# A transformer with two mixtures of experts: routing weights, expert table and destinations made in the tiles' blocks instead of the routers

## The chip, the cores and the metric

The kernel runs on one core of one Trainium2 chip. The time is the device time of one execution in microseconds (us). The engines are PE (TensorE, matrix products), DVE (VectorE), ACT (ScalarE), POOL (GpSimd) and SP (SyncE, which here only issues DMAs). Each engine runs its own row of instructions in order; they meet through semaphores.

## What is computed

Six residual layers on x, 64 sequences of 32 tokens of 256 values, T = 2048 tokens in all: cross attention with 16 heads, a gated recurrence, a mixture of experts (8 experts, the 2 best for each token, plus a shared one), cross attention with one head, causal attention, and a second mixture (16 experts, the 4 best, plus a shared one). The change is in the two mixtures alone:

```python
# first mixture, after a layer norm
logits = x @ Wg
probs = jax.nn.softmax(logits, axis=-1)
vals, idx = jax.lax.top_k(probs, TOP_K)                       # TOP_K = 2 of E = 8
weights = vals / (jnp.sum(vals, axis=-1, keepdims=True) + EPS)
...
act = jax.nn.silu(hpre)                                       # x @ W1[e] + b1[e]
out = jnp.einsum('te,teh->th', cw, y)                         # y = act @ W2[e] + b2[e]
out = out + SHARED_SCALE * shared
# second mixture, scores = sigmoid(logits)
_, tidx = jax.lax.top_k(masked, TOPK)                         # 4 of 16, from the 2 best groups of 4
w = jnp.take_along_axis(scores, tidx, axis=1)
w = w / (jnp.sum(w, axis=-1, keepdims=True) + 1e-20)          # times 2.5
...
hact = jax.nn.silu(g) * u * combine[:, :, None]
```

## The kernel before

P = 128 is the number of partitions, T = 2048 tokens are NT = 16 tiles of 128, D = 256 is the width, C = 2 its halves. The program is a row of stages, and a stage a row of blocks; at a block's end all engines meet. A mixture has four blocks.

**The boundary** (`boundary`) makes the layer norm, turns it for PE and stores its rows in DRAM (`n_rows`) for the gathers.

**The router** (`route`, L1000 to L1160) sorts tokens by expert. PE makes the logits. DVE makes, in `choose`, the best experts of each token (`r.choice`) and their weights (`r.w`): in the first mixture through ACT's exponential (L1709 to L1719), in the second by picking from the sigmoids (L2207 to L2224). Then, still on DVE and nearly all of it serial (each step signals `m_chain` and the next waits for it): which token has which expert (`hot`, L1082), how many tokens each expert has before and in this place (PE, L1041 and L1042), how many tiles of 128 rows each expert needs (`need`, L1103), where they end (`ends`, the scan of L1105) and begin (`begins`). From `ends` comes the **expert table** `r.expert` (L1110 to L1123): for each routed tile its expert, six of them packed in one integer. From `begins` and `place` comes each token's slot (L1114, L1125 to L1130), cut in tile (`hi_f`) and row (`lo_f`). A loop (L1143 on DVE, L1062 on ACT, L1049 on PE) places the token numbers into slots by one-hot products, and ACT copies the outcome into `halves`. From its differences `held` (L1146) DVE makes the token of each slot (`r.token`, L1153) and the **destinations** `r.dest` (L1148 to L1157): the row of `y_rows` in DRAM where that slot's result goes. The routed tiles number 39 in the first mixture and 79 in the second (`mix.tiles`).

**The tiles** (`first_tiles`, L1188; `second_tiles`, L1402). The loop runs over u = 0 to N-1: the first 16 tiles are the shared expert on the tokens in their order, the others are routed. Per tile PE multiplies up (`ascend`), ACT applies silu, DVE splits the hidden values in two halves of 16 bits (`split` in the first; `multiply`, `high`, `low` in the second), PE multiplies down (`descend`), DVE takes the result (`add` or `result`; L1567 for shared, L1571 for routed tiles of the second). In the second, PE also turns the hidden values (`flip`) and ACT copies them (`flipped`). PE runs ahead of DVE: `ascend(u + 2)` in the first and `ascend(u + 3)` in the second stand before `descend(u)`. Beside the shared tiles ACT and DVE split the experts' weights, which came by DMA during the router, slot by slot (`cast_high` L959, `cast_low` L965). In the second, DVE's order per tile is

```python
for u in range(N):
    if u + 3 < N:
        multiply(u + 3)
        high(u + 3)
        low(u + 3)
    result(u)
    for i in casts(u):
        slots.cast_low(dve, i)
```

and what ties PE to DVE there is, in `descend(u)`, the wait for the product's buffer of two tiles before, `pe.wait_ge(k.t_ycopied.sem, k.t_ycopied.at(u - 1))`, that is `result(u - 2)`.

POOL gathers the routed tiles' rows from `n_rows` (`gather`, L1371 and L1599), by `r.token`, and scatters results to `y_rows` (`scatter`, L1375 and L1603), by `r.dest`. In the first tiles it may be three gathers ahead, in the second 44: there it issues 44 gathers at the block's start before its first scatter. PE and ACT read `r.expert` into registers to find a routed tile's weights (`Experts`).

The combination then adds each token's results with the weights `r.w`.

## Time and profile before

| | |
|---|---|
| median of 3 runs | 1519.88 us (1517.51 to 1522.65) |
| the profiled execution | 1531.23 us |
| its span in the profile | 1529.2 us |
| PE busy (matmuls) | 1169.9 us, 77% of the span |
| DVE busy | 1031.0 us, 67% |
| ACT busy | 826.0 us, 54% |
| POOL busy | 435.7 us, 28% |
| mean granted clock of PE | 0.874 |

The profiled execution stands 11.35 us above the median; 2.0 us of it lie outside the span. An engine can be idle because it waits for another, and a row of the timeline says after its work in brackets how long the engine was idle before and who ended that ("issue": nothing that the profile shows; "remote": an unknown queue). PEclk is the granted clock as a share of 2.4 GHz.

### The profile page before, as it was taken

What the parts mean: (1) busy time and instruction counts of PE and PEld (TensorE: products, weight loads), DVE (VectorE), ACT (ScalarE), POOL (GpSimd) and SP (SyncE); (2) the same over time, 40 slices, a digit from 0 to 9 for tenths busy, and PEclk for the clock granted to TensorE, in tenths of its full rate; (3) what the DMA queues carried; (4) which work ended last, traced back from release to release, by engine and by line L of the source; (5) the groups of instructions that cost most, each with busy time, mean ns of one, the idle gap of its engine ahead of it and who ended that gap; (6) DMA issues with size and microseconds to landing.
All of it is one profiled execution on the core that took longest, in us unless ns stands there. A gap on an engine that the chain in (4) does not pass through costs nothing. (4 is left out here: it accounts for less than half of the span.)

```text
span 1529.2 us, 41178 instructions
## 1 busy us (share of the span) xinstructions
PE 1169.9 (77%) x13430; PEld 862.1 (56%) x13430; DVE 1031.0 (67%) x2885; ACT 826.0 (54%) x2163; POOL 435.7 (28%) x480
## 2 busy tenths in 40 slices
PE   4899999998798539999999927678723327787890
PEld 2688888886344429988888724235611215555660
DVE  5699999997647777966666545345779228454566
ACT  6688888885588546844444306127454125444450
POOL 0555555551200000023333202000200641555550
PEclk9999999999899759999999958789955659899895
DMA  2333333331000283011111169970160320222228
GB/s 95 99 78 80 82 76 81 81 82 64 1 1 1 91 318 155 2 57 47 51 50 51 37 204 321 348 234 1 66 255 28 87 65 19 73 76 78 78 69 281
DMA packets 111934, 151.45 MB, mean 99 GB/s; under 512 B 13632, under 2 KB 96960, under 8 KB 111680
## 3 DMA queue, kind: packets, MB, share of 16 engines
q1 hardware_dynamic: 95792, 114.11, 23.6%
q0 software_dynamic: 11328, 30.95, 6.6%
q10 hardware_dynamic: 4688, 4.72, 0.9%
q8 instruction: 78, 1.28, 0.4%
q14 instruction: 48, 0.39, 0.1%
HBM read 127.97 MB, written 21.76 MB: 98 GB/s over the span
## 5 line engine op out<-in xcount | busy, mean ns | idle before, releaser
L1291 ACT ACTIVATE mixture_and_attentions_h<-ps,mixture_and_attentions_b 128x128 f32<-128x128 f32 x440 | 125.3, 373 | 137.3 <-PE ps L1243 134.3
L1243 PE MATMUL ps<-xture_and_attentions_m_w 128*128 128x128 f16 x1872 | 156.2, 219 | 1.8 <-DVE xture_and_attentions_m_w L1319 1.7
L1243 PEld LDWEIGHTS ps<-xture_and_attentions_m_w 128*128 x1872 | 129.1, 98 | 37.1 <-issue 3.5
L648 POOL TENSOR_TENSOR ads_and_recurrence_ctx_s<-ads_and_recurrence_ctx_c,ads_and_recurrence_ctx_s 128x512 f16<-128x512 f32 x64 | 74.2, 1159 | 178.2 <-ACT ads_and_recurrence_ctx_s L577 178.2
L597 ACT ACTIVATE ads_and_recurrence_probs<-ps,s_and_recurrence_neg_max 128x257 f32<-128x257 f32 x256 | 117.7, 480 | 1.1 <-DVE s_and_recurrence_neg_max L679 1.1
L1261 PE MATMUL ps<-xture_and_attentions_m_w,ixture_and_attentions_hs 128*128 x312 | 117.5, 379 | 1.0 <-DVE xture_and_attentions_m_w L1344 1.0
L1599 POOL DMA_INDIRECT tage_second_mixture_rows<-n_rows,e_second_mixture_r_token x79 | 76.8, 973 | 133.7 <-POOLq L1002 110.0
L1475 PE MATMUL ps<-stage_second_mixture_m_w,stage_second_mixture_x_s 128*128 x474 | 98.5, 348 | 20.7 <-ACT stage_second_mixture_x_s L1517 13.9
L1603 POOL DMA_INDIRECT y_rows<-stage_second_mixture_y,ge_second_mixture_r_dest x79 | 77.1, 976 | 124.6 <-DVE stage_second_mixture_y L1571 114.5
L1371 POOL DMA_INDIRECT ture_and_attentions_rows<-n_rows,e_and_attentions_r_token x39 | 39.0, 999 | 258.1 <-POOLq L1002 159.6
L1327 DVE TENSOR_SCALAR ixture_and_attentions_hs<-mixture_and_attentions_h 128x512 f16<-128x512 f32 x110 | 47.6, 433 | 87.7 <-PE ps L1262 71.3
L1550 DVE SCALAR_TENSOR_TENSOR stage_second_mixture_h<-ps,stage_second_mixture_h 128x192 f32<-128x192 f32 x95 | 33.8, 355 | 97.5 <-ACT stage_second_mixture_h L1522 55.5
L688 DVE TENSOR_SCALAR _heads_and_recurrence_pn<-ads_and_recurrence_probs,heads_and_recurrence_inv 128x256 f32<-128x256 f32 x256 | 79.8, 371 | 8.3
L1262 PE MATMUL ps<-xture_and_attentions_m_w,ixture_and_attentions_hs 128*128 x312 | 85.0, 273 | 0.0
L679 DVE TENSOR_REDUCE s_and_recurrence_neg_max<-ps 128x2 f32<-128x514 f32 x128 | 81.8, 678 | 1.9 <-PE ps L519 1.9
L494 PE MATMUL ps<-ads_and_recurrence_ctx_s,currence_wh_L_xattn_wk_t 128*128 128x256 f16 x512 | 78.3, 276 | 5.1 <-issue 5.1
L1522 ACT ACTIVATE stage_second_mixture_h<-ps 128x192 f32<-128x192 f32 x95 | 31.4, 331 | 90.6 <-PE ps L1475 42.4
L1329 DVE SCALAR_TENSOR_TENSOR ixture_and_attentions_hs<-mixture_and_attentions_h,ixture_and_attentions_hs 128x512 f16<-128x512 f32 x110 | 76.3, 693 | 3.8
L527 PE MATMUL ps<-consts_sb,_heads_and_recurrence_pn 128*128 128x128 f32 x512 | 77.0, 273 | 2.2 <-DVE heads_and_recurrence_p_t L695 2.2
L1490 PE MATMUL ps<-stage_second_mixture_m_w,stage_second_mixture_h_t 128*128 (+1 forms) x95 | 27.4, 288 | 66.1 <-DVE x_sb L1567 30.9
L503 PE MATMUL ps<-currence_wh_L_xattn_wv_t,ads_and_recurrence_ctx_s 128*128 128x256 f16 x512 | 77.7, 275 | 0.0
L1375 POOL DMA_INDIRECT y_rows<-xture_and_attentions_m_w,re_and_attentions_r_dest x39 | 38.5, 986 | 132.6 <-DVE xture_and_attentions_m_w L1344 132.3
(401 smaller groups left out, 3371.9 us busy)
## 6 DMA issues: line engine op xcount, KB each, us to landing
ads_and_recurrence_ctx_t<-in_ctx_t SPq DMA_DIRECT2D x64, 257.0 KB, 2.7
e_and_attentions_b_ctx_t<-in_ctx_t SPq DMA_DIRECT2D x15, 1028.0 KB, 9.1
ure_and_attentions_b_ctx<-in_ctx SPq DMA_DIRECT2D x30, 512.0 KB, 8.9
xture_and_attentions_m_w<-in_m_w SPq DMA_DIRECT2D x2, 5632.0 KB, 37.3
ds_and_recurrence_mask_i<-in_mask SPq DMA_DIRECT2D x256, 32.1 KB, 1.7
tage_second_mixture_rows<-y_rows SPq DMA_DIRECT2D x16, 512.0 KB, 9.6
stage_second_mixture_m_w<-in_m_w SPq DMA_DIRECT2D x2, 3840.0 KB, 20.5
xture_and_attentions_m_w<-in_m_w SPq DMA_DIRECT2D x1, 5120.0 KB, 16.6
```

Of the source, the lines that this page charges most:

```text
L494: last = pe.matmul(ps[:, KB, m * KR:(m + 1) * KR], w[:, c, m * P:(m + 1) * P], x[:, c, :], start=(n_ == 0), stop=(n_ == len(products) - 1))
L503: last = pe.matmul(ps[:, VB, r * D:(r + 1) * D], x[:, c, r * P:(r + 1) * P], w[:, c, :], start=(n_ == 0), stop=(n_ == len(products) - 1))
L527: last = pe.transpose(ps[:, TB, j * P:(j + 1) * P], pn[p][:, j, r * P:(r + 1) * P], c_["ident"])
L597: act.activation(probs[p][:, j, :], ps[:, SB + j, 0:SK], ACT.Exp, bias=neg_max[:, p, j:j + 1], accum_out=sums[:, p, j:j + 1]).then_inc(k.a ...
L679: dve.tensor_reduce(neg_max[:, p, 2 * h:2 * h + 2], ps[:, SB + 2 * h:SB + 2 * h + 2, 0:SK], AX.X, ALU.max, negate=True).then_inc(k.a_max.s ...
L688: last = dve.tensor_scalar(pn[p][:, j, :], probs[p][:, j, 0:KR], inv[:, p, j:j + 1], None, ALU.mult)
L1243: last = pe.matmul(ps[:, UB + 2 * (u % 2) + f // PER, (f % PER) * P:(f % PER + 1) * P], slots.of(e, c, at, P), a[:, c, :], start=(n == 0), ...
L1261: pe.matmul(ps[:, YB + u % 2, 0:2 * D], h, slots.of(e, block, at, 2 * D), start=(f == 0), stop=False)
L1262: last = pe.matmul(ps[:, YB + u % 2, 0:D], l, slots.of(e, block, at, D), start=False, stop=(f == FC - 1))
L1291: last = act.activation(h32[n][:, at:at + P], ps[:, UB + 2 * (u % 2) + n, at:at + P], ACT.Silu, scale=1 / (WS * NS), bias=b1[:, bass.ds(e ...
L1475: last = pe.matmul(ps[:, UB + u % 2, 0:UP], a[:, c, :], weight(u, w, c * UP, UP), start=(n == 0), stop=(n == len(products) - 1))
L1603: pool.indirect_dma_start(k.y_rows, bass.IndirectOffsetOnAxis(ap=r.dest[:, s:s + 1], axis=0), y[s % Y][:, :], None).then_inc(k.t_stored[s ...
```

## The change

The weights `r.w`, the expert table `r.expert` and the destinations `r.dest` are no longer made in the router's block but in the tiles' block behind it. A class `Late` holds what passes from the one to the other and the scratch space. It lies in buffers that the tiles use only later: in the first mixture the two halves of the second hidden buffer (`second_hidden`, the `hs1` of `first_tiles`), in the second the 12 result buffers, now one tensor `y` made before the router. `ends` and `held` are written there by the router.

In the first tiles DVE makes the table before `split(0)`, and the destinations and the weights between `split(0)` and `split(1)`. In the second tiles it makes the table at u = 2, the destinations at u = 13 (`NT - 3`) and the weights at u = 14 (`NT - 2`), each between `low(u + 3)` and `result(u)`. A count `m_known` takes the place of `m_ranked`: 1 is the slots in the router, 2 the table (PE, ACT and, in the first mixture, DVE wait for it), 3 the destinations (POOL waits for it before its first scatter). In the router, DVE no longer waits for ACT's exponential; `place` is summed while `ends` is on its way; and the K products and K sums of `hot` with `place` (L1125, L1127) are one of each.

```diff
+RESULTS = 12
...
+class Late:
...
+        self.ends = self.part(0, E)
+        self.ends_le = self.part(0, NTL * E).rearrange("p (n e) -> p n e", e=E)
+        self.exp_f = self.part(0, NTL + AT_ONCE - 1)
+        self.packed = self.part(0, NTL)
+        self.held = self.part(1, K * NTL).rearrange("p (k n) -> p k n", n=NTL)
...
+    def experts(self, dve, r):
+        k, E, NTL = self.k, self.mix.E, self.mix.tiles
+        exp_f, packed = self.exp_f, self.packed
+        tile = k.c["iota"][:, 0:NTL].unsqueeze(2).broadcast_to([P, NTL, E])
+        dve.memset(exp_f, 0.0)
+        dve.tensor_tensor(self.ends_le, self.ends.unsqueeze(1).broadcast_to([P, NTL, E]), tile, ALU.is_le).then_inc(k.m_chain.sem, 1)
...
+        for j in range(AT_ONCE - 2, -1, -1):
+            digits = exp_f[:, AT_ONCE - 1:AT_ONCE - 1 + NTL] if j == AT_ONCE - 2 else packed
+            dve.scalar_tensor_tensor(packed, digits, float(E1), exp_f[:, j:j + NTL], ALU.mult, ALU.add).then_inc(k.m_chain.sem, 1)
+            dve.wait_ge(k.m_chain.sem, k.m_chain.next())
+        dve.tensor_copy(r.expert[:, :], packed).then_inc(k.m_known.sem, 1)
+
+    def destinations(self, dve, r):
...
+        dve.scalar_tensor_tensor(r.dest[:, :], row_f[:, 1, :], 1.0, row_f[:, 2, :], ALU.subtract, ALU.add).then_inc(k.m_known.sem, 1)
...
-def route(k, mix, wg, slots, scores, choose, r):
+def route(k, mix, wg, slots, scores, choose, r, late):
...
+        ends, held = late.ends, late.held
...
-            dve.tensor_tensor_scan(ends[:, :], ones_e[:, :], need[:, :], 0.0, ALU.mult, ALU.add).then_inc(k.m_chain.sem, 1)
-            dve.wait_ge(k.m_chain.sem, k.m_chain.next())
-            dve.tensor_tensor(begins[:, :], ends[:, :], need[:, :], ALU.subtract)
-
-            tile = c_["iota"][:, 0:NTL].unsqueeze(2).broadcast_to([P, NTL, E])
-            dve.tensor_tensor(ends_le[:, :, :], ends[:, :].unsqueeze(1).broadcast_to([P, NTL, E]), tile, ALU.is_le)
-            dve.tensor_tensor(place[:, :, :].rearrange("p e t -> p (e t)"), tmp[:, :, :].rearrange("p e t -> p (e t)"), ps[:, PB, 0:E * NT], ALU.add).then_inc(k.m_chain.sem, 1)
-            dve.wait_ge(k.m_chain.sem, k.m_chain.next())
-            dve.tensor_reduce(exp_f[:, 0:NTL], ends_le[:, :, :], AX.X, ALU.add)
+            dve.tensor_tensor_scan(ends, ones_e[:, :], need[:, :], 0.0, ALU.mult, ALU.add).then_inc(k.m_chain.sem, 1)
+            dve.tensor_tensor(place[:, :, :].rearrange("p e t -> p (e t)"), tmp[:, :, :].rearrange("p e t -> p (e t)"), ps[:, PB, 0:E * NT], ALU.add)
+            dve.wait_ge(k.m_chain.sem, k.m_chain.next())
+            dve.tensor_tensor(begins[:, :], ends, need[:, :], ALU.subtract).then_inc(k.m_chain.sem, 1)
+            dve.wait_ge(k.m_chain.sem, k.m_chain.next())
             dve.scalar_tensor_tensor(place[:, :, :], begins[:, :].unsqueeze(2).broadcast_to([P, E, NT]), float(P), place[:, :, :], ALU.mult, ALU.add).then_inc(k.m_chain.sem, 1)
...
-            for j in range(AT_ONCE - 2, -1, -1):
-                digits = exp_f[:, AT_ONCE - 1:AT_ONCE - 1 + NTL] if j == AT_ONCE - 2 else packed[:, :]
-                dve.scalar_tensor_tensor(packed[:, :], digits, float(E1), exp_f[:, j:j + NTL], ALU.mult, ALU.add).then_inc(k.m_chain.sem, 1)
-                dve.wait_ge(k.m_chain.sem, k.m_chain.next())
-            dve.tensor_copy(r.expert[:, :], packed[:, :])
-            for kk in range(K):
-                dve.tensor_tensor(hot[:, kk, :, :], hot[:, kk, :, :], place[:, :, :], ALU.mult).then_inc(k.m_chain.sem, 1)
-                dve.wait_ge(k.m_chain.sem, k.m_chain.next())
-                last = dve.tensor_reduce(slot_f[:, kk, :], hot[:, kk, :, :].rearrange("p e t -> p t e"), AX.X, ALU.add)
-            last.then_inc(k.m_chain.sem, 1)
+            dve.tensor_tensor(hot[:, :, :, :].rearrange("p k e t -> p k (e t)"), hot[:, :, :, :].rearrange("p k e t -> p k (e t)"),
+                              place[:, :, :].rearrange("p e t -> p (e t)").unsqueeze(1).broadcast_to([P, K, E * NT]), ALU.mult).then_inc(k.m_chain.sem, 1)
...
+            dve.tensor_reduce(slot_f[:, :, :], hot[:, :, :, :].rearrange("p k e t -> p k t e"), AX.X, ALU.add).then_inc(k.m_chain.sem, 1)
...
-            dve.tensor_tensor(held[:, :, :], halves[:, :, 1:NTS], halves[:, :, 0:NTL], ALU.subtract).then_inc(k.m_chain.sem, 1)
-            dve.wait_ge(k.m_chain.sem, k.m_chain.next())
-            dve.scalar_tensor_tensor(which[:, :, :], held[:, :, :], 0.5, c_["iota"][:, 0:K].unsqueeze(2).broadcast_to([P, K, NTL]), ALU.is_gt, ALU.mult)
...
-            dve.scalar_tensor_tensor(r.dest[:, :], row_f[:, 3, :], 1.0, row_f[:, 2, :], ALU.subtract, ALU.add)
+            dve.tensor_tensor(held, halves[:, :, 1:NTS], halves[:, :, 0:NTL], ALU.subtract).then_inc(k.m_chain.sem, 1)
+            dve.wait_ge(k.m_chain.sem, k.m_chain.next())
+            dve.tensor_reduce(row_f[:, :], held.rearrange("p k n -> p n k"), AX.X, ALU.add).then_inc(k.m_chain.sem, 1)
+            dve.wait_ge(k.m_chain.sem, k.m_chain.next())
+            dve.tensor_scalar(r.token[:, :], row_f[:, :], 1.0, 0.0, ALU.subtract, ALU.max)
...
+        hs = [[k.sb(f"hs0{x}", [P, F0], F16, ctx=ctx) for x in range(2)], second_hidden]
...
+                if f == PER and u + 3 == NT:
+                    pe.wait_ge(k.m_known.sem, k.m_known.at(2))
...
+                if u == NT:
+                    act.wait_ge(k.m_known.sem, k.m_known.at(2))
...
                 if s == 0:
                     dve.wait_ge(k.m_bias.sem, 32)
+                    dve.wait_ge(k.m_known.sem, k.m_known.at(2))
...
+            late.experts(dve, r)
             split(0)
+            late.destinations(dve, r)
+            late.weigh(dve)
...
+            pool.wait_ge(k.m_known.sem, k.m_known.at(3))
...
-        y = [k.sb(f"y{b}", [P, D], ctx=ctx) for b in range(Y)]
+        y = [results[:, b, :] for b in range(Y)]
...
+                if u + 4 == NT:
+                    pe.wait_ge(k.m_known.sem, k.m_known.at(2))
...
+                if u == 2:
+                    late.experts(dve, r)
+                if u == NT - 3:
+                    late.destinations(dve, r)
+                if u == NT - 2:
+                    late.weigh(dve)
...
+                if s == 0:
+                    pool.wait_ge(k.m_known.sem, k.m_known.at(3))
...
+            second_hidden = [k.sb(f"hs1{x}", [P, F0], F16, ctx=ctx) for x in range(2)]
+            late = Late(k, mix, [h[:, :].bitcast(F32) for h in second_hidden])
...
-            dve.tensor_tensor(ex[:, :, :], v8[:, :, :], v8[:, :, 0:1].broadcast_to([P, NT, 8]), ALU.subtract).then_inc(k.m_shift.sem, 1)
-            dve.wait_ge(k.m_expd.sem, k.m_expd.at(1))
-            dve.tensor_reduce(z[:, 0, :], ex[:, :, :], AX.X, ALU.add)
+            dve.tensor_tensor(ex, v8[:, :, :], v8[:, :, 0:1].broadcast_to([P, NT, 8]), ALU.subtract).then_inc(k.m_shift.sem, 1)
+
+        def weigh(dve):
+            dve.tensor_reduce(z[:, 0, :], ex, AX.X, ALU.add)
             dve.tensor_tensor(z[:, 2, :], ex[:, :, 0], ex[:, :, 1], ALU.add).then_inc(k.m_chain.sem, 1)
...
+            results = k.sb("y", [P, RESULTS, D], ctx=ctx)
+            flat, cut = results[:, :, :].rearrange("p b d -> p (b d)"), 1444
+            late = Late(k, mix, [flat[:, 0:cut], flat[:, cut:RESULTS * D]])
...
+        def weigh(dve):
             for n in range(K1):
                 last = dve.tensor_tensor(one[:, n, :, :], c_["iota"][:, 0:E1].unsqueeze(1).broadcast_to([P, NT, E1]), r.choice[:, :, n:n + 1].broadcast_to([P, NT, E1]), ALU.is_equal)
...
+        late.weigh = weigh
```

The loop of DVE that places the tokens, the gathers, the scatters and all work of PE are the same, and the number of instructions on PE, ACT and POOL too, but for the waits.

Three places of DVE's order show the move. The first is the end of the first router and the start of the first tiles. Before (`held`, `which`, `row_f` and `r_token`, `r_dest` as above, then two branches from block to block, then `split(0)`):

```order
L1146 TENSOR_TENSOR _mixture_and_attentions_held<-ixture_and_attentions_halves 128x78
L1148 SCALAR_TENSOR_TENSOR mixture_and_attentions_which<-_mixture_and_attentions_held,consts_sb 128x78
L1149 TENSOR_REDUCE mixture_and_attentions_row_f<-_mixture_and_attentions_held 128x39
L1151 TENSOR_REDUCE mixture_and_attentions_row_f<-mixture_and_attentions_which 128x39
L1152 SCALAR_TENSOR_TENSOR mixture_and_attentions_row_f<-mixture_and_attentions_row_f,consts_sb 128x39
L1153 TENSOR_SCALAR xture_and_attentions_r_token<-mixture_and_attentions_row_f 128x39
L1155 SCALAR_TENSOR_TENSOR mixture_and_attentions_row_f<-mixture_and_attentions_row_f 128x39
L1157 SCALAR_TENSOR_TENSOR ixture_and_attentions_r_dest<-mixture_and_attentions_row_f 128x39
L1002 UNCONDITIONAL_BRANCH
L1309 UNCONDITIONAL_BRANCH
L1327 TENSOR_SCALAR st_mixture_and_attentions_hs<-rst_mixture_and_attentions_h 128x512
L1329 SCALAR_TENSOR_TENSOR st_mixture_and_attentions_hs<-rst_mixture_and_attentions_h,st_mixture_and_attentions_hs 128x512
```

and now (`hs` is the second hidden buffer wherever it is not the target of L1359):

```order
L1181 TENSOR_TENSOR st_mixture_and_attentions_hs<-ixture_and_attentions_halves 128x78
L1183 TENSOR_REDUCE mixture_and_attentions_row_f<-st_mixture_and_attentions_hs 128x39
L1185 TENSOR_SCALAR xture_and_attentions_r_token<-mixture_and_attentions_row_f 128x39
L1056 UNCONDITIONAL_BRANCH
L1341 UNCONDITIONAL_BRANCH
L1022 MEMSET st_mixture_and_attentions_hs 128x44
L1023 TENSOR_TENSOR st_mixture_and_attentions_hs<-st_mixture_and_attentions_hs,consts_sb 128x312
L1025 TENSOR_REDUCE st_mixture_and_attentions_hs<-st_mixture_and_attentions_hs 128x39
L1027 TENSOR_SCALAR st_mixture_and_attentions_hs<-st_mixture_and_attentions_hs 128x39
L1031 SCALAR_TENSOR_TENSOR st_mixture_and_attentions_hs<-st_mixture_and_attentions_hs 128x39 x5
L1033 CAST ture_and_attentions_r_expert<-st_mixture_and_attentions_hs 128x39
L1359 TENSOR_SCALAR st_mixture_and_attentions_hs<-rst_mixture_and_attentions_h 128x512
```

The seven rows from `which` to `r_dest` have become two, and behind the branches the six rows of the expert table (L1022 to L1033) stand ahead of the first split.

The second place is in the second tiles, at u = 13 and 14. Before (L1550 to L1561 are the split of one tile, L1567 is a result):

```order
L1561 TENSOR_TENSOR stage_second_mixture_hs<-stage_second_mixture_h,stage_second_mixture_hs 128x64
L1567 SCALAR_TENSOR_TENSOR x_sb<-ps,x_sb 128x256
L1550 SCALAR_TENSOR_TENSOR stage_second_mixture_h<-ps,stage_second_mixture_h 128x192
L1555 CAST stage_second_mixture_hs<-stage_second_mixture_h 128x192
L1560 TENSOR_TENSOR stage_second_mixture_hs<-stage_second_mixture_h,stage_second_mixture_hs 128x128
L1561 TENSOR_TENSOR stage_second_mixture_hs<-stage_second_mixture_h,stage_second_mixture_hs 128x64
L1567 SCALAR_TENSOR_TENSOR x_sb<-ps,x_sb 128x256
```

and now, from the last row of the split of tile 16 to the result of tile 13:

```order
L1601 TENSOR_TENSOR stage_second_mixture_hs<-stage_second_mixture_h,stage_second_mixture_hs 128x64
L1038 TENSOR_REDUCE stage_second_mixture_y<-stage_second_mixture_y 128x79
L1039 SCALAR_TENSOR_TENSOR stage_second_mixture_y<-stage_second_mixture_y,consts_sb 128x316
L1041 TENSOR_REDUCE stage_second_mixture_y<-stage_second_mixture_y 128x79
L1042 SCALAR_TENSOR_TENSOR stage_second_mixture_y<-stage_second_mixture_y,consts_sb 128x79
L1044 SCALAR_TENSOR_TENSOR stage_second_mixture_y<-stage_second_mixture_y 128x79
L1046 SCALAR_TENSOR_TENSOR stage_second_mixture_r_dest<-stage_second_mixture_y 128x79
L1607 SCALAR_TENSOR_TENSOR x_sb<-ps,x_sb 128x256
```

The six instructions that make the destinations stand between the split and the result.

The third place is one tile on, from the last row of the split of tile 17 (the sixth row of the listing before):

```order
L1601 TENSOR_TENSOR stage_second_mixture_hs<-stage_second_mixture_h,stage_second_mixture_hs 128x64
L2263 TENSOR_TENSOR stage_second_mixture_y<-consts_sb,tage_second_mixture_r_choice 128x256 x4
L2267 TENSOR_TENSOR stage_second_mixture_y<-stage_second_mixture_y 128x256 x4
L2271 TENSOR_REDUCE stage_second_mixture_r_w<-stage_second_mixture_y 128x16 x4
L2274 TENSOR_REDUCE stage_second_mixture_y<-stage_second_mixture_r_w 128x16
L2276 TENSOR_SCALAR stage_second_mixture_y<-stage_second_mixture_y 128x16
L2278 RECIPROCAL stage_second_mixture_y<-stage_second_mixture_y 128x16
L2280 SCALAR_TENSOR_TENSOR stage_second_mixture_r_w<-stage_second_mixture_r_w,stage_second_mixture_y 128x64
L1607 SCALAR_TENSOR_TENSOR x_sb<-ps,x_sb 128x256
```

The weights' sixteen instructions stand ahead of the result of tile 14 (L1607).

## Rows read from the trace of the kernel before

**Rows 1.** Windows of the second tiles: stretch, length, each engine's busy us, PEclk, DMA.
```profile
1254.00:1280.00 26.00, 18.30 (x134) 11.81 (x132) 25.38 (x56) 18.65 (x30) 0.00 (x0) 0.95 0.00 1
1290.00:1484.00 194.00, 159.41 (x1325) 115.62 (x1323) 105.89 (x368) 94.01 (x222) 105.87 (x109) 0.92 0.23 75
```

**Rows 2.** Timeline of DVE in the first router: start, length, work [idle before].
```profile
555.94 0.28 DVE L1711 TENSOR_REDUCE mixture_and_attentions_z<-ixture_and_attentions_ex 128x16 f32<-128x128 f32 x1 [1.71 <-ACT ixture_and_attentions_ex L1702]
...
557.04 0.67 DVE L1082 TENSOR_TENSOR xture_and_attentions_hot<-consts_sb,_and_attentions_r_choice 128x128 f32<-128x128 f32 x2
...
560.26 0.17 DVE L1105 TENSOR_TENSOR_SCAN ture_and_attentions_ends<-re_and_attentions_ones_e,ture_and_attentions_need 128x8 f32<-128x8 f32 x1
...
563.45 0.28 DVE L1125 TENSOR_TENSOR xture_and_attentions_hot<-xture_and_attentions_hot,ure_and_attentions_place 128x128 f32<-128x128 f32 x1
...
573.39 0.24 DVE L1146 TENSOR_TENSOR ture_and_attentions_held<-re_and_attentions_halves 128x78 f32<-128x78 f32 x1 [0.58 <-ACT re_and_attentions_halves L1064]
...
574.79 0.20 DVE L1157 SCALAR_TENSOR_TENSOR re_and_attentions_r_dest<-ure_and_attentions_row_f 128x39 int32<-128x39 f32 x1
```

**Rows 3.** Timeline of DVE in the second router.
```profile
1146.45 1.43 DVE L2207 TENSOR_TENSOR stage_second_mixture_one<-consts_sb,_second_mixture_r_choice 128x256 f32<-128x256 f32 x4
...
1151.75 2.19 DVE L1082 TENSOR_TENSOR stage_second_mixture_hot<-consts_sb,_second_mixture_r_choice 128x256 f32<-128x256 f32 x4
...
1158.37 0.19 DVE L1105 TENSOR_TENSOR_SCAN tage_second_mixture_ends<-ge_second_mixture_ones_e,tage_second_mixture_need 128x16 f32<-128x16 f32 x1
...
1158.68 1.47 DVE L1110 TENSOR_TENSOR e_second_mixture_ends_le<-tage_second_mixture_ends,consts_sb 128x1264 f32<-128x1264 f32 x1
...
1164.08 0.41 DVE L1125 TENSOR_TENSOR stage_second_mixture_hot<-stage_second_mixture_hot,age_second_mixture_place 128x256 f32<-128x256 f32 x1
...
1167.98 0.19 DVE L1130 CAST ge_second_mixture_slot_i<-ge_second_mixture_slot_f 128x64 int32<-128x64 f32 x1
...
1185.95 0.49 DVE L1146 TENSOR_TENSOR tage_second_mixture_held<-ge_second_mixture_halves 128x316 f32<-128x316 f32 x1 [2.16 <-ACT ge_second_mixture_halves L1064]
...
1186.88 0.68 DVE L1149 TENSOR_REDUCE age_second_mixture_row_f<-tage_second_mixture_held 128x79 f32<-128x316 f32 x1
...
1188.85 0.24 DVE L1157 SCALAR_TENSOR_TENSOR ge_second_mixture_r_dest<-age_second_mixture_row_f 128x79 int32<-128x79 f32 x1
```

**Rows 4.** Timeline of the first tiles: three rows of DVE, then PE.
```profile
579.29 0.65 DVE L1327 TENSOR_SCALAR ixture_and_attentions_hs<-mixture_and_attentions_h 128x512 f16<-128x512 f32 x1 [4.30 <-ACT mixture_and_attentions_h L1291]
...
583.43 0.43 DVE L1327 TENSOR_SCALAR ixture_and_attentions_hs<-mixture_and_attentions_h 128x512 f16<-128x512 f32 x1 [0.50 <-ACT mixture_and_attentions_h L1291]
...
585.15 0.69 DVE L1329 SCALAR_TENSOR_TENSOR ixture_and_attentions_hs<-mixture_and_attentions_h,ixture_and_attentions_hs 128x512 f16<-128x512 f32 x1
...
588.62 0.50 PE L1243 MATMUL ps<-n,xture_and_attentions_m_w 128*128 128x128 f16 x6
```

**Rows 5.** DMA queues, 1190 to 1260 us: the larger of the two that carry instructions.
```profile
q8 instruction: 1, 0.02, 0.1%
```

**Rows 6.** Timeline of the second tiles, 1196 to 1256 us: PE, ACT, DVE.
```profile
1201.12 1.14 PE L1475 MATMUL ps<-stage_second_mixture_m_w,n 128*128 128x384 f16 x6
...
1247.12 0.33 ACT L1522 ACTIVATE stage_second_mixture_h<-ps 128x192 f32<-128x192 f32 x1 [27.78 <-issue]
...
1252.11 0.42 DVE L1567 SCALAR_TENSOR_TENSOR x_sb<-ps,x_sb 128x256 f32<-128x256 f32 x1 [3.51 <-remote]
1253.73 1.49 DVE L965 SCALAR_TENSOR_TENSOR stage_second_mixture_m_w<-stage_second_mixture_m_w 128x1280 f16<-128x1280 f32 x1 [1.19 <-ACT stage_second_mixture_m_w L959]
```

**Rows 7.** Timeline of the second tiles, 1266 to 1297 us: PE, then DVE.
```profile
1280.25 1.74 PE L1475 MATMUL ps<-stage_second_mixture_m_w,stage_second_mixture_x_s 128*128 x6 [2.79 <-DVE stage_second_mixture_m_w L965]
...
1288.80 0.27 PE L1490 MATMUL ps<-stage_second_mixture_m_w,stage_second_mixture_h_t 128*128 x1
...
1283.42 0.41 DVE L1567 SCALAR_TENSOR_TENSOR x_sb<-ps,x_sb 128x256 f32<-128x256 f32 x1
...
1286.41 0.42 DVE L1567 SCALAR_TENSOR_TENSOR x_sb<-ps,x_sb 128x256 f32<-128x256 f32 x1
```

94 lines of the change are left out of this document (52 added, 42 removed).

## Prediction

> **What bounds the kernel now.** I read the page first: the span is a long row of stages, with no engine busy all the time, so what a cut is worth has to be read stage by stage. Then I read the timeline of DVE (the vector engine) in the two routers. There the reader is to see one serial chain: each small instruction of DVE waits for the one before, and PE, ACT and POOL stand still until the router's block ends. So what leaves DVE's chain in a router shortens the program by its full length, as far as the tiles' block that follows can take the work in for nothing.
>
> In the first router, DVE waits 1.71 us for ACT's exponential, then makes the weights until 557.04; makes the table of experts between 560.26 and 563.45; and makes the destinations after 573.39 [rows 2]. In the second the same three pieces stand at 1146.45 to 1151.75, 1158.37 to 1167.98 and 1185.95 to the end of the last row, 1189.09 [rows 3].
>
> Third, the second tiles. POOL begins there with 44 gathers in a row, and in that time work moves only now and then: PE had finished the up-projection of tile 5 at 1201.12 + 1.14 = 1202.26, and ACT, idle for 27.78 us, took it at 1247.12. DVE, free from 1248.60, added the result of tile 2 at 1252.11, though nothing in the program but PE's signal was missing to it [rows 6]. I call this late signals: they come with the gathers and end with them. From 1254 to 1280 DVE is the bound, busy 25.38 of 26 us, for it splits one weight slot per tile. From 1290 on PE leads, with 159.41 of 194 us, and DVE has room (105.89) [rows 1].
>
> **The change, part by part, all on DVE's chain.**
>
> Weights, first router. The wait of 1.71 and the six instructions from 555.94 to 557.04, 1.10, leave: 2.8 us.
>
> Expert table, first router. From the scan (560.26) to the first product (563.45) are 3.19 us [rows 2]. What stays is the scan (0.17), the sum into place (as a 128-column instruction some 0.28, the second product's row), the difference (0.17) and the last fold into place (0.28), partly overlapped: 0.8. Gain 2.4.
>
> Destinations, first router. From 573.39 to 574.99 are 1.60; what stays is the difference (0.24), one sum (about as much) and the token (about 0.2), with hand-overs: 0.7. Gain 0.9. The fused product and sum of the first router I leave at nothing. First router: 2.8 + 2.4 + 0.9 = 6.1 us.
>
> Weights, second router: 1151.75 - 1146.45 = 5.3. Expert table: 1164.08 - 1158.37 = 5.7, of which the same four instructions stay, now 256 columns wide (0.41 each for the two large ones, 0.2 for the small): 1.1. Gain 4.6. Products and sums fused: eight instructions took 1167.98 - 1164.08 = 3.9. One product of 1024 columns is, by 1.47 us for 1264 columns, about 1.2; one sum over 1024 columns, by 0.68 for 316 less some 0.15 that every instruction costs, 1.7 ns a column, is about 1.9. Together 3.2, gain 0.7. Destinations: 1189.09 - 1185.95 = 3.1, of which 0.49 + 0.68 + 0.2 and hand-overs stay, 1.4. Gain 1.7 [rows 3]. Second router: 5.3 + 4.6 + 0.7 + 1.7 = 12.3 us. Both: 18.4 us.
>
> Now the other side, in the tiles' blocks.
>
> First tiles, expert table: some 2.7 us of DVE at the head of the block. DVE idles there 4.30 us before its first split at 579.29 [rows 4], so it costs nothing. If that cover were short, the first split would be late, and PE behind it.
>
> First tiles, destinations (1.4) and weights (1.1), between split 0 and split 1. Split 1 stood ready to start at 583.43 after 0.50 of idle, and ended at 585.15 + 0.69 = 585.84; it now begins 2.0 later and ends near 587.9. PE asks for it first at 588.62, when it starts tile 3 [rows 4]. Margin 0.7 us: nothing again, but thin.
>
> Second tiles, expert table at tile 2: two passes of 1.47, five small steps, the cast: 4.7 us. It stands behind the split of tile 5, where DVE was free at 1248.60 and waited 3.51 for PE's signal. So it ends at 1253.3, the result of tile 2 starts there instead of 1252.11, and the weight split after it, which waited for ACT until 1253.73 [rows 6], starts on time. Cost nothing. At its dearest (DVE cannot use that idle time, below) it costs 4.7 - 1.2 = 3.5, the 1.2 being the idle time before the weight split.
>
> Second tiles, destinations at tile 13 and weights at tile 14. DVE: the result of tile 13 moves from 1283.42 to 1285.9 (2.5 for the six instructions). The split of tile 17 follows and ends at 1287.7. Then come the weights, 5.3 long, so the result of tile 14 moves from 1286.41 to 1293.0. Who waits: PE's down-projection of tile 16, at 1288.80 before, needs the buffer that this result frees, so it starts at 1293.4 [rows 7]. That is 4.6 us on the path. Nothing gives it back, since afterwards PE leads again. And PE idle for 4.6 us will come back slow: after 2.79 us of idle at 1280.25 its six matmuls took 1.74 [rows 7], where the same six took 1.14 at 1201.12 [rows 6]. That is 0.6 for six of a tile's eighteen instructions; over the tile and part of the next I put 1.5. Payback 6.1 us. The bounds are 0 (the hold falls into a wait that comes anyway) and 7.8 + 1.5 = 9.3 (all of DVE's 7.8 us lands on PE); I take 6.1 since the hand-overs of [rows 7] give it.
>
> New waits. PE and ACT wait for the expert table before reading it, at tile 13 and 16 of their loops, long after it is there. POOL waits for the destinations behind its first gathers: in the second tiles they are there near 1286, and the first result to scatter is tile 16's, whose down-projection began at 1288.80 [rows 7]. Queued behind that wait is POOL's whole second half, but it does not wait longer. DMAs are neither added nor removed; the loads of weights still have the shared tiles as cover. Instructions on PE, ACT and POOL stay the same.
>
> **Sum:** 18.4 - 6.1 = 12.3 us. The profiled execution took 1531.23 us, 11 more than the median; it would come to 1518.9, and the median of 1519.88 to 1507.6. A measurement can tell about 0.3%, 4.6 us, from no change.
>
> **Rivals.**
>
> A, *the payback is not paid*. From 1290 to 1484 PE is idle 194 - 159.41 = 34.6 us already [rows 1]; a hold at tile 16 may merely stand in for such waits. Then the gain is 18.4 and the time 1501.5. Against it: at 1288.80 PE ran without a gap.
>
> B, *the expert table is paid for*. ACT's long wait before 1247.12 has no releaser, only "issue", and DVE's a "remote" one [rows 6]. If these were not late signals of PE but engines without code, DVE could not run the table in its idle time, and 3.5 more is lost: 8.8 gained, 1511.1. Rows against it: in 70 us the larger of the two queues that carry instructions moved one packet [rows 5], and the engines pass only some tens of instructions there, so they can hardly have wanted more. 
> C, *slower*: POOL bunches. In the routed tiles POOL issues 109 indirect DMAs, 105.87 us busy [rows 1], and PE's 34.6 idle us are, as with the first gathers, time in which signals come late behind DMAs issued back to back. After DVE's hold at tile 14, POOL has several results pending and issues them in one burst, gathers between; the pattern could lock in. It cancels the gain when PE's idle time there grows from 34.6 to 47; grown by half again, to 52, the kernel is 5 us slower, 1525. Against it: the hold is about two tiles long, and DVE, with room, spreads results at PE's pace again.
>
> D, *it does not do what it says*: the router gets shorter, but the late signals after the gathers take the gain back, as they come in gaps of any size. Between the forecast and C: about 1519, no difference.
>
> **How the numbers follow.** Forecast 0.54 (its own range 1505 to 1511), A 0.18, B 0.16, D 0.07, C 0.05. The range takes in A and B with the unknown of a few us in the late signals: 1500.5 to 1514; it leaves out D, C and the tails of the others. Faster by over 0.3% are the forecast, A and B, 0.88; within 0.3% D, 0.07; slower C, 0.05.
>
> **What would show it.** Router blocks shorter by 6.1 and 12.3 us (from DVE's first instruction to PE's first matmul in the tiles). First tiles: PE without a gap near tile 3, a gap if the margin of 0.7 was wrong. Second tiles: the expert table in the idle time before the result of tile 2; a gap of PE of 4 to 5 us before the down-projection of tile 16, and slow matmuls behind it; PE's idle time afterwards near 34.6. The prediction is wrong if that gap is missing (A), if the table starts only once the late signal arrives (B), or if the later idle time has grown by 12 us or more (C, D).

## The result, and the profile after

The changed kernel takes 1511.25 us (median of 13 runs, 1502.03 to 1518.49) against 1523.86 for the kernel before (13 runs beside it): ratio 0.9921, interval 0.9901 to 0.9941. In a ratio that is 12.0 us less, 12.3 were forecast. Two more comparisons, each of the same two kernels on one chip, gave 0.9921 (0.9893 to 0.9949) and 0.9923 (0.9900 to 0.9947). Of the executions reported below one, of e2_weights_in_router, was slow (1833.43 us) and is left out, so that its median is that of the other six. The profiled execution took 1505.64 us (span 1503.5, clock 0.881), 5.6 less than the median; the one before took 1531.23, 7.4 more than 1523.86, so the two spans differ by 25.7 us, twice what the change is worth. I therefore compare stretch by stretch.

**First router.** Timeline of DVE of the changed kernel, against [rows 2]:

```profile
554.59 0.29 DVE L1759 TENSOR_TENSOR ixture_and_attentions_hs<-mixture_and_attentions_v 128x128 f32<-128x128 f32 x1
554.79 0.68 DVE L1130 TENSOR_TENSOR xture_and_attentions_hot<-consts_sb,_and_attentions_r_choice 128x128 f32<-128x128 f32 x2
...
558.02 0.17 DVE L1153 TENSOR_TENSOR_SCAN ixture_and_attentions_hs<-re_and_attentions_ones_e,ture_and_attentions_need 128x8 f32<-128x8 f32 x1
...
558.82 0.42 DVE L1160 TENSOR_TENSOR xture_and_attentions_hot<-xture_and_attentions_hot,ure_and_attentions_place 128x256 f32<-128x256 f32 x1
...
568.52 0.24 DVE L1181 TENSOR_TENSOR ixture_and_attentions_hs<-re_and_attentions_halves 128x78 f32<-128x78 f32 x1 [0.58 <-ACT re_and_attentions_halves L1113]
...
569.06 0.18 DVE L1185 TENSOR_SCALAR e_and_attentions_r_token<-ure_and_attentions_row_f 128x39 int32<-128x39 f32 x1
```

`hot` (L1130) follows the subtraction that ACT's exponential needs (L1759), without the wait of 1.71 us for its outcome. From the scan to the first product are 558.82 - 558.02 = 0.80 us, where 3.19 were; that is the 0.8 forecast. The end is three instructions (L1181 to L1185) in place of eight.

**Second router**, against [rows 3]:

```profile
1141.11 2.19 DVE L1130 TENSOR_TENSOR stage_second_mixture_hot<-consts_sb,_second_mixture_r_choice 128x256 f32<-128x256 f32 x4
...
1147.73 0.19 DVE L1153 TENSOR_TENSOR_SCAN stage_second_mixture_y<-ge_second_mixture_ones_e,tage_second_mixture_need 128x16 f32<-128x16 f32 x1
...
1148.82 1.22 DVE L1160 TENSOR_TENSOR stage_second_mixture_hot<-stage_second_mixture_hot,age_second_mixture_place 128x1024 f32<-128x1024 f32 x1
1150.08 1.86 DVE L1163 TENSOR_REDUCE ge_second_mixture_slot_f<-stage_second_mixture_hot 128x64 f32<-128x1024 f32 x1
1151.97 0.20 DVE L1165 CAST ge_second_mixture_slot_i<-ge_second_mixture_slot_f 128x64 int32<-128x64 f32 x1
...
1169.95 0.49 DVE L1181 TENSOR_TENSOR stage_second_mixture_y<-ge_second_mixture_halves 128x316 f32<-128x316 f32 x1 [2.16 <-ACT ge_second_mixture_halves L1113]
...
1171.19 0.20 DVE L1185 TENSOR_SCALAR e_second_mixture_r_token<-age_second_mixture_row_f 128x79 int32<-128x79 f32 x1
```

From scan to product are 1.09 us (forecast 1.1), and the fused product and sum take 1151.97 - 1148.82 = 3.15 (forecast 3.2). From `held` to the end of the tokens are 1171.39 - 1169.95 = 1.4 (forecast 1.4).

**First tiles**, against [rows 4], DVE and then PE:

```profile
569.59 0.10 DVE L1022 MEMSET ixture_and_attentions_hs<- 128x44 f32 x1 [0.34 <-PEq L1056]
...
573.55 0.65 DVE L1359 TENSOR_SCALAR ixture_and_attentions_hs<-mixture_and_attentions_h 128x512 f16<-128x512 f32 x1 [1.36 <-ACT mixture_and_attentions_h L1323]
...
579.10 0.42 DVE L1359 TENSOR_SCALAR ixture_and_attentions_hs<-mixture_and_attentions_h 128x512 f16<-128x512 f32 x1
...
580.61 0.69 DVE L1361 SCALAR_TENSOR_TENSOR ixture_and_attentions_hs<-mixture_and_attentions_h,ixture_and_attentions_hs 128x512 f16<-128x512 f32 x1
```
```profile
569.55 7.97 PE L1271 MATMUL ps<-n,xture_and_attentions_m_w 128*128 128x128 f16 x102 [1.34 <-PEq L1056]
...
582.32 0.50 PE L1271 MATMUL ps<-n,xture_and_attentions_m_w 128*128 128x128 f16 x6
```

The expert table begins the block and is done before ACT's first hidden values are there: 1.36 us of the idle 4.30 are left. Split 1 ends at 581.30, which is 11.8 us behind PE's first matmul of the block (569.5); before it ended 10.5 behind it (585.84 against 575.3). It is late by 1.2 us, not 2.0. PE starts tile 3 at 582.32, without a gap, 1.0 us behind the end of the split; the forecast had left a margin of 0.7.

**Second tiles, expert table** (DVE, against [rows 6]):

```profile
1197.81 0.13 DVE L1022 MEMSET stage_second_mixture_y<- 128x84 f32 x1
1197.85 1.41 DVE L1023 TENSOR_TENSOR stage_second_mixture_y<-stage_second_mixture_y,consts_sb 128x1264 f32<-128x1264 f32 x1
...
1202.49 0.20 DVE L1033 CAST _second_mixture_r_expert<-stage_second_mixture_y 128x79 int32<-128x79 f32 x1
1202.61 0.41 DVE L1607 SCALAR_TENSOR_TENSOR x_sb<-ps,x_sb 128x256 f32<-128x256 f32 x1
```

It runs in one piece of 4.8 us, and the result of tile 2 follows at once. Whether that result had waited for the table this profile alone doesn't tell. In the two later profiles of the same kernel (e6 and e12 below) it had not: the table was ready 13.08 and 11.61 us before PE's signal came. DVE of e12:

```profile
1210.85 0.20 DVE L1033 CAST _second_mixture_r_expert<-stage_second_mixture_y 128x79 int32<-128x79 f32 x1
1222.65 0.42 DVE L1607 SCALAR_TENSOR_TENSOR x_sb<-ps,x_sb 128x256 f32<-128x256 f32 x1 [11.61 <-issue]
```

**Second tiles, the hold** (DVE, then PE, against [rows 7]):

```profile
1255.73 0.68 DVE L1038 TENSOR_REDUCE stage_second_mixture_y<-stage_second_mixture_y 128x79 f32<-128x316 f32 x1
...
1258.15 0.42 DVE L1607 SCALAR_TENSOR_TENSOR x_sb<-ps,x_sb 128x256 f32<-128x256 f32 x1
...
1259.50 1.42 DVE L2263 TENSOR_TENSOR stage_second_mixture_y<-consts_sb,_second_mixture_r_choice 128x256 f32<-128x256 f32 x4
...
1264.79 0.42 DVE L1607 SCALAR_TENSOR_TENSOR x_sb<-ps,x_sb 128x256 f32<-128x256 f32 x1
```
```profile
1265.44 0.27 PE L1528 MATMUL ps<-stage_second_mixture_m_w,stage_second_mixture_h_t 128*128 x1 [4.24 <-DVE x_sb L1607]
...
1266.21 1.87 PE L1513 MATMUL ps<-stage_second_mixture_m_w,stage_second_mixture_x_s 128*128 x6
...
1268.20 0.42 PE L1528 MATMUL ps<-stage_second_mixture_m_w,stage_second_mixture_h_t 128*128 x1
```

The result of tile 14 comes at 1264.79, and PE's down-projection of tile 16 has stood idle for 4.24 us for it (forecast 4.6). Behind it six matmuls take 1.87 us instead of 1.14 and single ones 0.42 instead of 0.27: the slow matmuls that the forecast priced at 1.5.

**Windows** of the changed kernel (columns as in [rows 1]):

```profile
1267.00:1461.00 194.00, 161.13 (x1348) 117.09 (x1346) 106.96 (x378) 95.05 (x225) 108.04 (x110) 0.94 0.24 75
```

In the 194 us from the first routed result on PE is idle 194 - 161.13 = 32.9 us; it was 34.6.

### The profile page after: what moved, and what is told of

It is laid out like the page before. It is cut to its first block and busy times, and to the rows that moved or that the text cites. A ratio compares the mean times of both kernels' runs of the same rounds, so it can differ in the third digit from the quotient of the medians.

```text
span 1503.5 us, 41174 instructions
## 1 busy us (share of the span) xinstructions
PE 1176.2 (78%) x13430; PEld 863.7 (57%) x13430; DVE 1028.3 (68%) x2879; ACT 825.8 (55%) x2163; POOL 440.9 (29%) x480
## 5 line engine op out<-in xcount | busy, mean ns | idle before, releaser
L1645 POOL DMA_INDIRECT tage_second_mixture_rows<-n_rows,e_second_mixture_r_token x79 | 79.9, 1012 | 119.4 <-POOLq L1056 95.7
L1407 POOL DMA_INDIRECT ture_and_attentions_rows<-n_rows,e_and_attentions_r_token x39 | 39.9, 1024 | 252.3 <-POOLq L1056 153.8
L1513 PE MATMUL ps<-stage_second_mixture_m_w,stage_second_mixture_x_s 128*128 x474 | 97.1, 344 | 11.1 <-ACT stage_second_mixture_x_s L1557 4.2
L1359 DVE TENSOR_SCALAR ixture_and_attentions_hs<-mixture_and_attentions_h 128x512 f16<-128x512 f32 x110 | 47.3, 430 | 82.1 <-PE ps L1290 71.0
## 6 DMA issues: line engine op xcount, KB each, us to landing
stage_second_mixture_m_w<-in_m_w SPq DMA_DIRECT2D x2, 3840.0 KB, 24.9
```

Source lines behind the costliest of these rows:

```text
L1513: last = pe.matmul(ps[:, UB + u % 2, 0:UP], a[:, c, :], weight(u, w, c * UP, UP), start=(n == 0), stop=(n == len(products) - 1))
L1645: pool.indirect_dma_start(rows[s % R][:, :], None, k.n_rows, bass.IndirectOffsetOnAxis(ap=r.token[:, s:s + 1], axis=0)).then_inc(k.t_rows[ ...
```

## The experiments

Two of the twelve kernels are the changed kernel itself and one is the kernel before; the others are edits of the changed kernel. They ran on three chips, which I call A (e1 to e4), B (e5 to e8) and C (e9 to e12). On A the kernel before takes 1435 us, on B 1528, on C 1526; the two first profiles look like those of B and C. The changed kernel without an edit did not run on A. The table gives stretches of the profiled executions in us, each from the start of one row of the timeline to the start of another: the first router (to PE's first matmul of the tiles), the first tiles (to PE's last up-projection), the stages between, the second router, then the second tiles in three pieces: from PE's first matmul to DVE's last split of a weight slot, from there to the first routed result, and from there to the last. One stretch is uneven between executions of the same kernel: to the last split the changed kernel took 79.1 us once and 86.7 and 86.2 later.

| kernel (chip) | router 1 | tiles 1 | between | router 2 | to last split | to first routed | routed | median, ratio to before |
|---|---|---|---|---|---|---|---|---|
| before, first profile | 31.2 | 300.0 | 250.1 | 64.0 | 89.1 | 11.7 | 198.7 | |
| changed, first profile | 24.8 | 299.7 | 252.2 | 50.3 | 79.1 | 16.7 | 195.6 | 1511.25, 0.9921 |
| e1_train (A) | 24.9 | 298.6 | 255.2 | 50.5 | 51.0 | 12.8 | 145.2 | 1422.58, 0.9908 |
| e2_weights_in_router (A) | 24.9 | 298.7 | 249.5 | 55.5 | 43.9 | 11.7 | 145.1 | 1422.47, 0.9918 |
| e3_table_in_routers (A) | 27.3 | 299.4 | 253.0 | 56.5 | 38.8 | 16.1 | 145.9 | 1423.86, 0.9922 |
| e4_paced (A) | 24.8 | 298.0 | 252.5 | 50.2 | 42.8 | 17.2 | 146.0 | 1419.22, 0.9896 |
| e5_before (B) | 31.2 | 299.3 | 251.3 | 64.1 | 86.7 | 11.6 | 198.7 | 1530.53, 1.001 |
| e6_changed (B) | 24.8 | 299.5 | 253.8 | 51.6 | 86.7 | 17.0 | 199.9 | 1516.13, 0.9921 |
| e7_spread (B) | 24.9 | 299.6 | 253.9 | 50.5 | 85.4 | 13.9 | 197.5 | 1512.92, 0.9906 |
| e8_spread_paced (B) | 24.8 | 299.6 | 251.2 | 51.6 | 64.0 | 12.9 | 198.7 | 1490.16, 0.9748 |
| e9_first_only (C) | 24.8 | 299.8 | 250.3 | 62.7 | 86.4 | 11.7 | 197.1 | 1519.66, 0.9964 |
| e10_slow_pace (C) | 24.8 | 299.2 | 252.7 | 51.7 | 51.1 | 15.2 | 202.5 | 1483.31, 0.9725 |
| e11_fewer_first (C) | 24.8 | 299.4 | 252.8 | 50.2 | 48.5 | 12.0 | 221.3 | 1496.99, 0.9821 |
| e12_changed (C) | 24.8 | 299.3 | 252.3 | 51.6 | 86.2 | 16.8 | 193.2 | 1512.32, 0.9923 |

Each ratio has an interval of about 0.002 to either side (e7: 0.987 to 0.9943).

### Chip A: where to put the pieces

**e1_train**

```diff
-                if u == 2:
+                if u == 1:
                     late.experts(dve, r)
-                if u == NT - 3:
+                if u == 2:
                     late.destinations(dve, r)
-                if u == NT - 2:
+                if u == 3:
                     late.weigh(dve)
```

> The changed kernel with the three late pieces of the second tiles moved earlier: expert table at u = 1, destinations at u = 2, weights at u = 3, all in the time of the first gathers, where DVE idles for many us. Forecast's theory (the hold of tile 16 by destinations and weights costs about 6 us: a gap of PE of 4.24 us measured, plus 1.5 us at half clock): the gap before the down-projection of tile 16 shrinks to under 1 us, and the time comes to about 6 us under the changed kernel, ratio to the kernel before about 0.988. Rival A (the hold stands in for waits that come anyway): the gap goes, but the block from PE's first matmul to the last result stays as long, ratio 0.992. Rival B (DVE's idle time in the gather train can't be used, since it has no code): the pieces push the train's end back by up to 12 us less the 6, ratio 0.994 or more.

Measured: ratio 0.9908 (0.9886 to 0.993). The hold is gone, 12.8 us from the last split to the first routed result, but the stretch ahead of it has 51.0 where e2, without the weights and with the destinations at tile 13, has 43.9. The ratio lies between the forecast's 0.988 and rival A's 0.992 and tells neither from the other; why, e3 shows.

**e2_weights_in_router**

```diff
             top8(k, dve, masked, v8, i8, r.choice)
+            weigh(dve)
...
-        late.weigh = weigh
+        late.weigh = lambda dve: None
```

> The changed kernel with the weights of the second mixture made in the router again, the rest as changed. Forecast's theory: the router is 5.3 us longer; in the tiles the result of tile 14 is late by only 2.5 - so PE's gap before the down-projection of tile 16 goes and with it about 4.2 + 1.5 us: the sum is about zero, ratio 0.992 as the changed kernel. So the move of the weights is worth nothing net. Rival A (payback not paid): 5.3 us slower than the changed kernel, ratio 0.9956.

Measured: 0.9918 (0.9898 to 0.9939). The router has 55.5 us, 5.3 more than e4; the last stretch of the shared tiles has 11.7, where e3 and e4, which make the weights at tile 14, have 16.1 and 17.2. The move of the second mixture's weights, placed where the change puts them, is worth 5.3 us less 4.4 (e3) to 5.5 (e4), which is about nothing. The ratio is the one expected (0.992); rival A's 0.9956 is outside the interval.

**e3_table_in_routers**

```diff
             dve.tensor_tensor(begins[:, :], ends, need[:, :], ALU.subtract).then_inc(k.m_chain.sem, 1)
             dve.wait_ge(k.m_chain.sem, k.m_chain.next())
+            late.experts(dve, r)
...
                 if u == 2:
-                    late.experts(dve, r)
+                    late.signal(dve)
```

The same stands in the first tiles. `signal` is one memset that gives `m_known`'s signal in the table's place.

> The changed kernel with the expert table made in both routers again (serially, in front of the fold into place); a single memset signals in the tiles at its place. Forecast's theory: the table costs nothing in the tiles, so this is slower by its whole length, 4.7 us in the second and 2.7 us in the first router: 7.4 us, ratio 0.997. Rival B (the table is paid for in the gather train, up to 3.5 us): slower by 3.9 us only, ratio 0.9947.

Measured: 0.9922 (0.9902 to 0.9942), where the forecast's theory said 0.997 and rival B 0.9947: both fail. The first router is 2.5 us longer and the second about 6, but the stretch to the last split is 38.8 against e2's 43.9: on this chip the table costs 5.1 us in the tiles, its full length. Neither theory had the reason. The timeline of DVE (e1, from tile 0's result on) has it:

```profile
1183.16 0.35 DVE L1590 SCALAR_TENSOR_TENSOR stage_second_mixture_h<-ps,stage_second_mixture_h 128x192 f32<-128x192 f32 x1
1184.24 0.13 DVE L1022 MEMSET stage_second_mixture_y<- 128x84 f32 x1
...
1191.80 0.68 DVE L1038 TENSOR_REDUCE stage_second_mixture_y<-stage_second_mixture_y 128x79 f32<-128x316 f32 x1
...
1196.97 1.43 DVE L2263 TENSOR_TENSOR stage_second_mixture_y<-consts_sb,_second_mixture_r_choice 128x256 f32<-128x256 f32 x4
...
1202.26 0.42 DVE L1607 SCALAR_TENSOR_TENSOR x_sb<-ps,x_sb 128x256 f32<-128x256 f32 x1
1202.59 1.48 DVE L966 SCALAR_TENSOR_TENSOR stage_second_mixture_m_w<-stage_second_mixture_m_w 128x1280 f16<-128x1280 f32 x1
...
1205.02 0.42 DVE L1607 SCALAR_TENSOR_TENSOR x_sb<-ps,x_sb 128x256 f32<-128x256 f32 x1
```

No row here has a bracket: DVE is never idle, one shared tile takes it 1205.02 - 1202.26 = 2.76 us, and the late signals of [rows 6] don't exist. So DVE is the bound from the first result to the last split, and every piece put there is paid: e1 has all three there, e3 none, and their stretches differ by 51.0 - 38.8 = 12.2 us, for pieces of 4.7 + 2.5 + 5.3 = 12.5.

**e4_paced**

```diff
+                    if s == 0:
+                        pool.wait_ge(k.t_ycopied.sem, k.t_ycopied.at((gathered - 8) // 3))
                     gather(gathered)
```

> The changed kernel with POOL's first 44 gathers of the second tiles paced: gather g waits until (g - 8) // 3 shared results are there. Theory of late signals (they are late because POOL issues gathers back to back): PE, ACT and DVE go through the shared tiles without long idle times, the 74 us from PE's first matmul to the first turn of a routed tile (of which DVE's own work is some 55) shrink by 10 to 20 us, and the kernel is faster by that, ratio 0.98 to 0.985, unless gathers that come later hold PE. Rival (the engines stand for code or for the weights' DMA, not for POOL): the 74 us stay, within their run-to-run spread of some 10 us, and the ratio stays 0.992 or gets worse since gathers come late.

Measured: 0.9896 (0.9877 to 0.9916). To the last split 42.8 us against 43.9 of e2, which has the same work there: pacing gives 1 us at most, not the 10 to 20 expected. With no late signals to remove, this says nothing of the theory yet.

### Chip B: both kernels once more, and pacing

**e5_before** is the kernel before and **e6_changed** the changed kernel, unedited.

> The kernel before, once more, for its trace beside the others. The four runs ahead of this one took some 1420 us, and the kernel before 1435: in their traces the shared tiles of the second mixture run without late signals, DVE busy from end to end while it splits weights (one tile in 2.76 us), and PE is never idle in the routed tiles. I expect the same here: first router 31, second router 64 us; from PE's first matmul of the tiles to the first routed result some 51 us (where the first profile had 101), routed results in 145 us. Theory of the bound DVE (below): second router and tiles up to the first routed result together 115 us. If late signals are back, 165.

> The changed kernel, once more. Theory of the bound DVE: without late signals DVE is the bound of the shared tiles from tile 0 to 12, so the expert table there (4.7 us) costs its full length, and destinations and weights at tiles 13 and 14 cost most of theirs (7.8): only the first router's 6.1, the fused steps and what the tail's slack hides remain. Second router 50.3, from PE's first matmul to the first routed result some 60 us, together 110.5 against 115 of before; ratio 0.992. Forecast's account (table free, hold 6.1): that stretch grows by 6.1 us only, the sum 108, ratio 0.990.

Measured: on this chip late signals are back: 98.3 us from PE's first matmul to the first routed result in e5 (86.7 + 11.6), 198.7 for the routed ones. The changed kernel has 86.7 us to the last split, as before to 0.1: the table is free here. The hold makes 17.0 of 11.6, and PE's row at tile 16 is

```profile
1275.61 0.37 PE L1528 MATMUL ps<-stage_second_mixture_m_w,stage_second_mixture_h_t 128*128 x1 [3.33 <-DVE x_sb L1607]
```

Here the forecast's account holds (hold 5.4, forecast 6.1); the theory of the bound DVE is one for chip A.

**e7_spread**

```diff
+    def pieces(self, dve, r):
+        def all_of():
+            yield from self.destinations(dve, r)
+            yield from self.weigh(dve)
+        return all_of()
...
-                if u == NT - 3:
-                    late.destinations(dve, r)
-                if u == NT - 2:
-                    late.weigh(dve)
+                if u == NT - 4:
+                    pieces = late.pieces(dve, r)
+                    next(pieces)
+                if NT - 4 <= u < NT:
+                    next(pieces, None)
+                    next(pieces, None)
+                if NT <= u < NT + 6:
+                    for _ in range(3):
+                        next(pieces, None)
                 result(u)
```

(`destinations` and `weigh` yield ahead of each of their instructions.)

> The changed kernel with destinations and weights of the second tiles cut in single instructions: two of them before the result of each tile from 12 to 15, three from tile 16 to 20, where DVE no longer splits weights and has some 0.5 us of room per tile. Both theories say that the hold of tile 16 goes: no gap of PE over 1.5 us before the down-projection of tiles 15 to 18, and 3 to 5 us less than the changed kernel, ratio 0.989. If the pieces are paid wherever they stand (DVE, not the hold, is what costs), no difference from the changed kernel.

Measured: 0.9906 (0.987 to 0.9943), 3.2 us under e6 by the medians, with the stretch after the last split down from 17.0 to 13.9 and no wait of PE for a result. The interval is too wide to tell 3 us from none; by that stretch 3 of the 5 us of the hold are got back.

**e8_spread_paced** has e7's edit and e4's.

> As e7_spread, and POOL's first 44 gathers paced as in e4_paced. Where no signals are late, pacing has nothing to give: as e7_spread, within 2 us. Where they are late, and the theory of back-to-back gathers holds, 10 to 20 us faster than e7_spread.

Measured: 0.9748 (0.9721 to 0.9774), 22.8 us under e7. To the last split 64.0 us against 85.4. The windows of e7 and e8, from PE's first matmul to the first routed result:

```profile
1174.00:1273.00 99.00, 48.72 (x300) 30.19 (x299) 51.04 (x129) 33.47 (x59) 44.66 (x44) 0.71 0.22 59
```
```profile
1172.00:1249.00 77.00, 49.49 (x298) 30.96 (x299) 50.88 (x129) 33.41 (x59) 49.21 (x44) 0.77 0.28 76
```

All engines do the same work in 77 us that took them 99, and POOL issues the same 44 gathers. Only when they are issued differs, so the late signals come from the gathers' bunch.

By itself this doesn't exclude engines that wait for code, since a paced POOL also leaves room on the DMA engines for code to come. The DMA queues do. In e6 no packet of an instruction queue, and none of the weights, moved from 1180 to 1240 us:

```profile
DMA packets 1969, 5.38 MB, mean 90 GB/s; under 512 B 657, under 2 KB 657, under 8 KB 1969
q0 software_dynamic: 1969, 5.38, 33.4%
```

All 1969 packets are the gathers' (`software_dynamic`). Yet waits of ACT of 13.81 and 16.59 us and of PE of 17.60 and 14.97 us ended in these 60 us. What ended them was not code that arrived. In e12 the same holds from 1180 to 1235.

### Chip C: half of the change, and how far pacing goes

**e9_first_only**

```diff
             dve.wait_ge(k.m_chain.sem, k.m_chain.next())
+            if mix.n == 1:
+                late.experts(dve, r)
...
             dve.tensor_scalar(r.token[:, :], row_f[:, :], 1.0, 0.0, ALU.subtract, ALU.max)
+            if mix.n == 1:
+                late.destinations(dve, r)
...
             top8(k, dve, masked, v8, i8, r.choice)
+            weigh(dve)
...
-                if u == 2:
-                    late.experts(dve, r)
-                if u == NT - 3:
-                    late.destinations(dve, r)
-                if u == NT - 2:
-                    late.weigh(dve)
+                if u in (2, NT - 3):
+                    late.signal(dve)
```

> The changed kernel with all three pieces of the second mixture made in its router again (table ahead of the fold into place, destinations behind the tokens, weights behind the choice); the first mixture as changed. Forecast's account: first router 6.1 us shorter than before, the second about as before, its tiles without the hold: 6 to 7 us faster than the kernel before, ratio 0.996. So the second mixture's part of the change is worth the other 6 us. Theory that the second mixture's part is worth nothing (DVE is the bound wherever it is put): ratio 0.992, as the changed kernel.

Measured: 0.9964 (0.9945 to 0.9982), as the forecast's account says. Its second router has 62.7 us, e12's 51.6: 11.1 for the three pieces, forecast 5.3 + 4.6 + 1.7 = 11.6. Of those, the hold takes 16.8 - 11.7 = 5.1 back, and to the last split both have the same (86.4 and 86.2). The medians differ by 1519.66 - 1512.32 = 7.3 us, for 6.0 by these stretches.

**e10_slow_pace** and **e11_fewer_first**, on top of e7:

```diff
+                    if s == 0:
+                        pool.wait_ge(k.t_ycopied.sem, k.t_ycopied.at((gathered - 6) // 2 if gathered < 36 else 15))
                     gather(gathered)
```
```diff
-                while gathered < min(R - 4 + (mix.tiles - R + 4) * (s + 1) // (mix.tiles - 20), mix.tiles):
+                while gathered < min(24 + (mix.tiles - 24) * (s + 1) // (mix.tiles - 20), mix.tiles):
+                    if s == 0:
+                        pool.wait_ge(k.t_ycopied.sem, k.t_ycopied.at((gathered - 6) // 2))
                     gather(gathered)
```

> As e8_spread_paced, with a slower pace: gather g waits for (g - 6) // 2 shared results, the last eight for 15. In e8 POOL fell behind its pace and issued back to back from 1190 to 1228 us, with waits of PE of 3.7 to 7.3 us in it. Theory of late signals: at 2 gathers per tile of 2.8 us POOL has gaps, PE's long waits in the shared tiles go, and the time from PE's first matmul to the first routed result comes from 77 down to 60 to 70 us, if the chip is one with late signals (ratio 0.966 to 0.972). Rival (the pace matters little, e8's gain came from the first waits alone): as e8, 0.975. On a chip without late signals: as e4_paced, 0.989 less the spread's 2 us.

> As e10_slow_pace, but with 24 gathers ahead of the first scatter in place of 44 (24, then 55 among the 79 scatters). If an indirect DMA delays signals by the same amount wherever it is issued, the shared tiles win some 10 us more and the routed tiles lose as much: as e10. If it costs less among scatters (POOL has room there), 5 to 10 us under e10. If the routed tiles are bound by POOL's 1.28 us per indirect DMA, they lose 20 times 1.28 = 26 us, and it is slower than e10 by 15 or more.

> The changed kernel, as the reference of the three others on this chip. Ratio 0.992 if signals are late here; if not, the theory of the bound DVE gives 0.99 to 0.993 as well, since what the table costs there (4.7) is about what the hold costs with late signals.

**e12_changed** is the changed kernel: 0.9923 (0.9900 to 0.9947). **e10** has 0.9725 (0.9698 to 0.9751), 29 us under the changed kernel and the lowest ratio of all, just above the expected 0.966 to 0.972. By the ratio it can't be told from e8 (0.9748, on chip B), but from PE's first matmul to the first routed result it takes 66.3 us, within the expected 60 to 70, where e8 takes 76.9; its routed part is 3.8 us longer. **e11** has 0.9821 (0.9795 to 0.9847). The windows of the two, shared tiles and then routed ones:

```profile
1172.00:1238.00 66.00, 45.06 (x301) 28.37 (x301) 50.51 (x128) 31.82 (x56) 44.77 (x40) 0.85 0.30 77
1238.00:1441.00 203.00, 157.92 (x1345) 115.46 (x1345) 111.88 (x392) 96.01 (x226) 113.17 (x117) 0.94 0.25 76
```
```profile
1172.00:1233.00 61.00, 45.58 (x306) 29.20 (x307) 50.62 (x130) 33.95 (x60) 27.54 (x24) 0.85 0.18 53
1233.00:1454.00 221.00, 169.09 (x1342) 120.40 (x1339) 111.89 (x390) 94.84 (x223) 128.71 (x131) 0.89 0.25 79
```

Twenty gathers moved from ahead of the first scatter to between the scatters: the shared tiles win 66.3 - 60.5 = 5.8 us, the routed ones lose 221.3 - 202.5 = 18.8, 0.94 us for each gather moved (1.2 if one goes by the windows, which have 24 gathers in place of 40 in the first stretch). That is more than the 0.3 us that it cost in its old place, so the first expectation and the second fail. e11 is 13.7 us slower than e10, near the third's 15 or more, but not for its reason: POOL is busy 128.71 of 221 us, so it isn't the bound. PE's busy time grew by 11.2 us with the lower clock (0.89 against 0.94), and its idle time by 7.

## Why the prediction was right

The gain and the larger parts of it were right, and the parts were then measured one by one. The absolute number needs care: the forecast of 1507.6 us counted from 1519.88, the median of 3 runs, and the measured 1511.25 is the very time that rival B had (1511.1). But beside the changed kernel the kernel before took 1523.86, so the gain is 12.0 us, not B's 8.8. The interval of the gain runs from 9.0 to 15.1 us, so that the time alone barely excludes B; the profiles do.

**First router, 6.1:** 31.2 - 24.8 = 6.4 us, the same in all profiles, and e9, which has this part and, of the second router, only the fused and reordered steps, has 0.9964, 5.5 us of 1525.73. **First tiles, nothing:** 299.7 against 300.0. The margin of 0.7 us at tile 3 was not used up: the split was late by 1.2 and not 2.0.

**Second router, 12.3:** 13.7 in the first pair of profiles, 12.5 in e5 and e6. Profiles of the changed kernel have either 50.2 to 50.5 or 51.6 to 51.7 us there; I have not looked for the cause of that one us. By parts: weights 5.3 (e2 against e4, 55.5 - 50.2), all three pieces 11.1 (e9 against e12) for 11.6, fusing and reordering 1.4 (e5 against e9, on two chips) for 0.7.

**Expert table at tile 2, nothing:** in e6 and e12 the table is ready 13.08 and 11.61 us before the signal for the result of tile 2 comes. The stretches agree, 86.7, 86.7, 86.4 and 86.2 us to the last split in e5, e6, e9 and e12, of which e6 and e12 have the table there; alone they would prove little, as the first pair has 89.1 and 79.1. Rival B is out, and with it the reading that the Trainium skill's page (Runtime: NRT & Kernel Launch, Instruction fetch mechanics) would have given to these idle times: pacing the gathers takes 21.4 us of them away (e8), and they end while no code arrives (e6). The prediction's own argument against B was weaker than it said: from 1190 to 1260 us PE alone passes 114 matmuls and 114 weight loads, not some tens of instructions, and the other instruction queue moved a packet too. What the page states of fetching itself no run here shows or denies.

**The hold, 6.1:** the stretch from the last split to the first routed result grew by 5.0, 5.4 and 5.1 us in the three pairs. The gap was 4.24, 3.33 and 4.32 us of PE, for 4.6. The forecast had the right place and instruction, and 1 us too much. The weights alone make it: e2 (on chip A), with the destinations still at tile 13, has 11.7, like the kernel before, so of the 7.8 us of both the destinations' 2.5 are free.

**Rival A** is out by the time: its 18.4 us lie beyond the intervals of all three comparisons, which reach to 15.1, 16.3 and 15.3 us. Whether a part of the hold comes back in the routed tiles stays open: they were 3.1 and 3.9 us shorter than in the kernel or edit without the hold in two pairs, and 1.2 longer in the third.

**Rivals C and D:** the routed tiles took 195.6, 199.9 and 193.2 us against 198.7, 198.7 and e9's 197.1: PE's idle time in the first pair's windows is 32.9 us for 34.6, so no pattern locked in, and nothing was eaten.

**The sum** of e5 to e6: -6.4 + 0.2 + 2.5 - 12.5 + 0 + 5.4 + 1.2, 9.6 us, with 0.4 after the last routed result and 0.9 ahead of the first router 10.9, the difference of the spans. The term that I had not is the stages between the mixtures, 2 us longer in most profiles of the changed kernel and its edits (251.2 to 255.2) than in e5, e9 and e2 (251.3, 250.3, 249.5). Their code is the same. It may be chance of an execution; that stays open. So it is in part luck that the forecast of 12.3 met the measured 12.0: in this pair the routers gave 0.5 us more than forecast and the hold cost 0.7 less, and the stages between, which the forecast had at nothing, took 2.5 back. The runs' medians, of 6 to 17 executions, give 11.9 to 13.4.

**One step holds on two of the three chips.** "Cost nothing" for the table rests on late signals, as the prediction said, which idle DVE at tile 2. On chip A they are missing, and the same table costs 5.1 us. The ratio would hardly differ there (e4, the changed kernel but for the pacing, has 0.9896), but a sum worked out from a trace of chip A would have had other terms: table 5, and idle time of none.

## What to carry to other kernels

Work moved off a serial chain is paid in the place where it lands by that place's own bound: it is free where the engine is idle for a reason that stays, costs its whole length where that engine leads, and behind a result that frees another engine's buffer it costs its length less the slack (5 of 7.8 us here). Cut in single instructions and spread over tiles that have room, it cost 3 us less than in one block, by the stretch if not yet by the time (e7). And if a long row of indirect DMAs stands ahead of a block in which other engines hand over often, try to issue them at the pace of that block's results: with the spread it gave 29 us on chip C, more than twice what the whole change gave, and on chip A 1 us at most.

## What the runs showed of the hardware

**The lateness of signals depends on the chip.** The same kernel takes 1435 us on A and 1526 to 1530 on B and C. Routers and first tiles take the same there to 2 us, though POOL issues 78 indirect DMAs in the 300 us of the first tiles; the difference is in the second tiles, where they are denser. Their routed part, windows of e4 (A) and e6 (B):

```profile
1230.00:1376.00 146.00, 145.58 (x1362) 110.98 (x1359) 107.19 (x379) 98.11 (x226) 109.71 (x113) 1.00 0.32 103
```
```profile
1278.00:1478.00 200.00, 163.76 (x1361) 117.88 (x1359) 106.72 (x379) 94.59 (x225) 110.12 (x112) 0.94 0.23 74
```

POOL issues the same 112 or 113 DMAs, of the same busy time (109.71 and 110.12 us), in 146 us on A and in 200 on B. On A PE is idle for 0.4 us and at the full clock, on B for 36 us and at 0.94. Waits of two stretches of 140 us in the routed part, of e4 (A) and of e12 (C) (us in total, times, the longest):

```profile
ACT stage_second_mixture_x_s L1557 <- PE ps L1501: 15.5, 69, 0.2
DVE stage_second_mixture_h L1590 <- ACT stage_second_mixture_h L1562: 30.6, 72, 0.5
```
```profile
ACT stage_second_mixture_x_s L1557 <- PE ps L1501: 22.7, 23, 3.2
DVE stage_second_mixture_h L1590 <- ACT stage_second_mixture_h L1562: 47.1, 35, 4.3
```

ACT's wait for PE's transposes was 0.2 us at most on A and up to 3.2 on C. One of these late signals by itself, PE and ACT of e12:

```profile
1313.01 0.33 PE L1521 MATMUL ps<-ident_h,stage_second_mixture_hs 128*128 128x128 f16 x3
...
1314.81 0.49 ACT L1567 ACTIVATE stage_second_mixture_h_t<-ps 128x384 f16<-128x384 f16 x1 [1.13 <-PE ps L1521]
```

The last transpose ended at 1313.34 and ACT took it 1.47 us later, after 1.13 us of idle time; nothing else was missing to it. The first router, in which POOL issues nothing, takes 24.8 or 24.9 us on all three chips in the changed kernel and its edits that leave it alone. What differs between the chips, the runs don't tell. Nor do they tell what in an indirect DMA holds the signals up, POOL's issuing or the transfer; only its timing was varied.

**Its price depends on the place.** On B and C pacing took 21.4 us (e7 to e8) and, with the spread, some 35 (e12's 86.2 against e10's 51.1) out of the stretch to the last split, down to 51 us where chip A has 43 to 44, though the number of gathers was the same. Moved in between scatters each costs some 1 us of the end (e11).
